# Attention of a transformer layer: half of the next sequence's value projection placed ahead of the first weighted values of a slot

## The reference

```python
x = x + 0.5 * ffn(layernorm(x))
x = x + attention(layernorm(x))
x = x + 0.5 * ffn(layernorm(x))

# attention: 16 query heads, 8 key/value heads, head size 32
q, k, v = X @ Wq, X @ Wk, X @ Wv          # then rotary embedding on q and k
att = 50 * tanh((q @ k.T) * 256**-0.5 / 50)
att = softmax(where(causal, att, -inf))
y = (att @ v) @ Wo
```

## Time and profile before

| | |
|---|---|
| median of 3 runs | 1027.0 us (1026.89 to 1028.26) |
| profiled execution | 1027.73 us |
| its span | 1026.0 us |
| TensorE matmuls busy | 939.1 us (92%) |
| TensorE weight loads | 694.0 us (68%) |
| VectorE, ScalarE, GpSimd | 626.0, 521.2 and 472.7 us |
| mean granted clock of TensorE | 0.979 |

### The profile page before, as it was taken

How to read it: one execution, slowest core, us unless ns; L and a number is a source line. 1 busy time by engine, 2 the same in 40 slices (tenths; PEclk the granted TensorE clock), 3 DMA queues, 4 the chain that set the end, 5 groups by cost and what they waited for, 6 DMA issues and landing times. The chain is left out here.

```text
span 1026.0 us, 17887 instructions
## 1 busy us (share of the span) xinstructions
PE 939.1 (92%) x6146; PEld 694.0 (68%) x6146; DVE 626.0 (61%) x1637; ACT 521.2 (51%) x765; POOL 472.7 (46%) x534
## 2 busy tenths in 40 slices
PE   2999998999999489999999999977999989999997
PEld 1788876777778456565666556635888767777786
DVE  4888777544444456665665676545988776453435
ACT  3766742132233257776777677655676622231322
POOL 5333203556542075776577567613512224555640
PEclk9999999999999799999999999988999999999999
DMA  5434235778774300000100100013323265777835
GB/s 186 118 96 126 67 95 150 172 179 184 174 172 104 123 1 22 21 21 31 31 20 21 41 20 21 11 62 94 94 84 111 68 175 133 170 182 180 181 58 170
DMA packets 95432, 101.90 MB, mean 99 GB/s; under 512 B 18688, under 2 KB 86656, under 8 KB 95360
## 3 DMA queue, kind: packets, MB, share of 16 engines
q1 hardware_dynamic: 83072, 83.17, 27.0%
q0 software_dynamic: 12288, 17.83, 10.4%
HBM read 65.44 MB, written 35.54 MB: 98 GB/s over the span
## 5 line engine op out<-in xcount | busy, mean ns | idle before, releaser
L80 PE MATMUL gu<-x_hi,gu_hi 128*128 128x512 f32 x308 | 139.9, 454 | 4.8 <-DVE act_gu L1124 4.8
L82 PE MATMUL gu<-x_lo,gu_hi 128*128 128x512 f32 x308 | 123.1, 400 | 0.0
L81 PE MATMUL gu<-x_hi,gu_lo 128*128 128x512 f32 x308 | 122.5, 398 | 0.0
L1603 POOL TENSOR_SCALAR_AFFINE_SELECT probs_at<-probs_at 128x1024 f32<-128x1024 f32 x64 | 70.5, 1102 | 110.8 <-ACT probs_at L1538 110.8
L1530 ACT ACTIVATE capped_at<-scores_at 128x2048 f32<-128x2048 f32 x64 | 93.1, 1454 | 45.1 <-PE scores_at L1438 44.9
L671 POOL DMA_INDIRECT rows<-z_rows,slots x64 | 68.9, 1077 | 75.4 <-DVE slots L1115 56.5
L957 ACT CAST a_hi<-act_gu 128x512 fp32r<-128x512 f32 x96 | 59.2, 616 | 83.1 <-DVE act_gu L1124 62.2
L1538 ACT ACTIVATE probs_at<-capped_at 128x2048 f32<-128x2048 f32 x64 | 95.2, 1487 | 2.0
L80 PE MATMUL down<-down_hi,a_hi 128*128 128x256 f32 x300 | 93.7, 312 | 0.2 <-DVE a_lo L1134 0.2
L867 PE MATMUL zT<-w_gu,xT 128*128 128x352 f32 x256 | 86.3, 460 | 0.0
L1005 ACT ACTIVATE y<-gu,rows 128x256 f32<-128x256 f32 x64 | 30.3, 474 | 109.9 <-PE gu L887 95.9
(11 more groups left out here) (220 smaller groups left out, 2403.3 us busy)
## 6 DMA issues: line engine op xcount, KB each, us to landing
w_gu<-in_w_gate SPq DMA_DIRECT2D x64, 176.0 KB
w_gu<-in_w_up SPq DMA_DIRECT2D x64, 176.0 KB
w_down<-in_w_down SPq DMA_DIRECT2D x64, 176.0 KB
z_rows<-z SPq DMA_DIRECT2D x16, 512.0 KB, 3.1
acc<-base SPq DMA_DIRECT2D x10, 512.0 KB, 3.6
out<-base SPq DMA_DIRECT2D x10, 512.0 KB, 4.0
x_f<-in_X SPq DMA_DIRECT2D x8, 512.0 KB, 4.7
xn_at<-acc SPq DMA_DIRECT2D x16, 256.0 KB, 2.8
```

Source lines behind the costliest of these rows:

```text
L80: nc.tensor.matmul(out, w_hi, x_hi, start=first, stop=False)
L81: nc.tensor.matmul(out, w_lo, x_hi, start=False, stop=False)
L82: return nc.tensor.matmul(out, w_hi, x_lo, start=False, stop=last)
L1603: pool.affine_select(out=diag, in_=diag, compare_op=ALU.is_ge, fill=zero, base=0, pattern=[[0, JH], [0, REP], [1, P]], channel_multiplier= ...
```

## The change

`project` takes the chunks that it is to make, both by default, and signals `piece_ready` only with the last one. In `slot_of`, chunk 0 of the values (six of twelve matmuls) is made between `score_unit(b, q, 1)` and `weighted_values(b, q, 0)`, chunk 1 where the whole was before. Both calls wait for `turned_ready`. This goes for every slot with a next sequence, 0 to 14. The projection of sequence 0 ahead of the slots is as before.

```diff
-            def project(b, q, n):
+            def project(b, q, n, halves=(0, 1)):
 
                 bank = pj[PIECE_BANK[n]]
                 if n == 0:
@@
                     pe.wait_ge(aT_lo_ready, b + 1)
                 elif n >= 2:
                     pe.wait_ge(turned_ready, b * PIECES + (2 if n == 2 else 1))
-                for c in range(2):
+                for c in halves:
                     for k in range(KC):
@@
-                last.then_inc(piece_ready, 1)
+                if halves[-1] == 1:
+                    last.then_inc(piece_ready, 1)
@@
                 score_unit(b, q, 1)
+                if ahead:
+                    project(b + 1, 1 - q, 3, (0,))
                 weighted_values(b, q, 0)
                 score_unit(b, q, 2)
                 if ahead:
                     project(b + 1, 1 - q, 2)
-                    project(b + 1, 1 - q, 3)
+                    project(b + 1, 1 - q, 3, (1,))
                 weighted_values(b, q, 1)
```

## The result

| | before | after |
|---|---|---|
| median | 1026.99 us (4 runs, 1026.89 to 1028.26) | 1019.04 us (4 runs, 1017.6 to 1021.42) |
| ratio to before | | 0.9922, 95% interval 0.9899 to 0.9945 |
| profiled execution | 1027.73 us | 1017.60 us |
| its span | 1026.0 us | 1015.8 us |
| mean granted clock | 0.979 | 0.980 |

The kernel became 8.0 us faster by the medians, where 8.5 was forecast (1018.5). The two profiled executions differ by 10.2 us of span. Behind these three numbers stand a part that hardly varies, the time from the first S1 to that of slot 15, and parts around it that do.

A forecast was written before the change was run, and what follows sets the result against it. TensorE's wait for GpSimd's mask ahead of unit 0's weighted values was taken to set the slot period. Loop slots 7.4, slots 13 and 14 0.9, slot 0 0.2: 8.5 us less, forecast 1018.5 us, range 1016.0 to 1022.5.

The forecast's parts named there:

- Spacing 0.118: Value matmuls in the projection block start every 0.118 us, so taking six out shortens that block by 0.70 us.
- W0 behind S1: Weighted values of unit 0 start 1.54 us behind score unit 1's start; before, 1.48 in the loop, 1.28 in written-out slots.
- The split's 0.2: Entry and exit of the moved block, two changes of matmul shape on TensorE, cost 0.2 us together.
- Both added waits at 0: Both halves' waits for VectorE's turn of piece 0 cost nothing; the turn ends 0.5 us early.
- A loop slot: Each of slots 1 to 12 gets 0.62 us shorter, 7.4 us in all.
- Slots 13 and 14: The two slots written out behind the loop gain 0.44 us each, 0.9 us together.
- Slot 0: First slot, without output projection: 0.70 us falls into an existing mask wait; ScalarE's earlier taking of values gains 0.2 us.
- Rival (b): Granted-clock dips around attention's end last longer or shorter: 1.3 to 2.5 us either way, 1016.0 to 1021.0 us; chance 0.06.
- (a): Rival: each change of shape around the moved half costs a whole matmul, 0.28 us; time 1023.3 us; chance 0.10 with its smaller form.
- its smaller form: The loop's 0.2 us of exposed waits ahead of unit 0's weighted values stays unhidden: 2.4 us less gain, 1020.9 us.
- (c): Rival: no gain, freed time becomes another wait in the slot, say for unit 2's mask; 1027.0 us; chance 0.03.
- (d): Rival: the moved half waits for VectorE's second turn, each slot loses 0.23 us; 1030.2 us; chance 0.05.

The follow-up runs named there:

- e4: Mask of unit 0 on two of four heads, in the kernel before: 1017.04 us beside 1024.45 us for the kernel before; loop period 19.77 us.
- e5: Mask of unit 0 on two of four heads, in the changed kernel: 1016.25 us beside 1024.83 us for the kernel before; loop period 19.59 us.
- the second measurement: The changed kernel again in more runs beside the kernel before: 1017.66 against 1024.93 us, ratio 0.9928.
- e3: Changed kernel with the six split-off matmuls put behind weighted values of unit 0: 1032.00 us beside 1024.45 us before; loop period 20.42 us.
- e6: Changed kernel whose moved half waits for VectorE's second turn too: 1032.65 us beside 1024.83 us for the kernel before; loop period 20.45 us.
- e2: Changed kernel with nine value matmuls moved instead of six: 1019.53 us beside 1024.45 us for the kernel before; loop period 19.59 us.
- e7: Changed kernel with the moved half ahead of score unit 1: 1022.39 us beside 1024.83 us for the kernel before; loop period 19.80 us.

## Why the prediction was right

**What bounds.** W0's wait for the mask set the period. This was read from 0.77 of idle and from the comparison of loop and written-out slots; e4 and e5 show it directly. The prediction also read the granted clock as full over all of attention but the last slot. That holds for the slots. Just ahead of them, where the projections of sequence 0 run, it was 0.60 in the changed kernel (355 to 362) and 0.66 before (355 to 364), so for the most part at the lower level. Both kernels have this, and it changed nothing in the sum.

**The terms.** Spacing 0.118 and six of them 0.70: P2 to W1 fell by 0.72. W0 behind S1: 1.54 worked out, 1.56 measured. These two are 0.02 off each and cancel. The split's 0.2: measured alone as 0.19 to 0.20. Both added waits at 0: the timeline has no idle time for them. A loop slot: 0.62 taken, 0.64 to 0.65 measured. I had taken 0.02 off for the mask's signal and the array's end falling together, and there was no such cost; over twelve slots that is 0.3 us. Slots 13 and 14: 0.44 each worked out, 0.45 measured.

**Slot 0** was the mis-sized term: 0.2 put, 0.44 measured. I counted ScalarE's 0.18 of idle ahead of taking the values. Without the wait, the instruction also starts before the end of the exponential (379.24 against 377.42 + 1.91 = 379.33), and the next one follows after 0.47 instead of 0.65: ScalarE's chain gained 0.45 (from the end of the exponential to the next tanh 0.83 before, 0.38 after).

**The sum** of the slots: 8.5 forecast, 9.08 measured, 0.3 from the loop's term and 0.24 from slot 0.

**The total.** 8.5 forecast, 8.0 by the medians, 7.3 in the second measurement. The forecast was as near as it was because the slots gave more and the ends gave some back. That is in part luck, as nothing in the prediction ties the one to the other. Rival (b), the clock, was no alternative with a chance of 0.06 but a part of the total of every pair: beyond the slots' 9.1 the profiled pair has another 1.1 in favour (0.45 of it ahead of attention), and the medians are 1.1 and 1.8 short of it. The range held all four runs (1017.6 to 1021.42); its lower end had 1 us for the clock, and its upper end was drawn for (a), not for the clock.

**The rivals.** (a) falls by e3, and its smaller form (the 0.2 of the loop not hidden) by the timeline of the changed kernel, where W0 is 1.56 behind S1 in the loop and in slot 13 alike. (c) didn't occur: no wait in the slot took the place of the one removed. (d) had the price right: e6, with the turn 1.3 later, is 0.22 a slot slower than before (0.23 worked out). Its threshold, a turn 1.1 us later, was not run; that W0 moved one for one with the half (0.85) agrees with it.

## What to carry to other kernels

When one engine has one wait in a loop, first find in the trace two rounds in which it differs and see whether the period differs by as much; then the gain of filling it is the time to be filled less what the split costs, and moving more than fits brings nothing more (e2). The time to be filled is read from starts: S1 to W0 is 1.48, S1's own matmuls need 0.64, so 0.84 was free, and less the 0.2 of the split that is the 0.64 measured. The 0.77 in the brackets, counted from the end of the row before, would have given 0.57. Look at who must have read the buffer that the moved work writes: that is the new wait, and its slack is the risk. Judge such an edit by the length of the loop in the trace, as the total of a run also carries clock changes elsewhere, here some microseconds.

## What the runs showed that I had not expected

- The entry of a block (0.22 us to the second matmul instead of 0.118) is also paid when TensorE resumes the same shape after a stall of 0.28 us (e7).
- The mask on half of the elements took 0.64 us instead of 1.10: by an estimate from these two, 0.18 of it doesn't shrink with the size.
- Matmuls whose result nobody reads, 52 of them in TensorE's waits at the end of attention, made the changed kernel 3.7 us faster. The granted clock in slot 15 stayed at 1.00, where without them it was at 0.57 in a stretch of it.
